# One exponential per score, eight buffers for exponentials and halves, values three double steps behind the scores, and second-layer statistics moved into the first layer's loop

## What is computed

```python
h = W.T[x] + b + positions
# first layer: 8 heads of 16 features, normalised dot products without softmax
t = layernorm(h); q, k, v = t @ w_qkv
dots = causal(q @ k.T * scale)
mu, s = mean and mean square of each causal row
h = h + ((dots - mu) * rsqrt(s + eps) * g + b) @ v @ w_out + b_out
# second layer: 2 heads of 64 features, and 8 experts of width 512
u = layernorm(layernorm(h), ln_g, ln_b)
q, k = l2norm(u @ Wq) * 8 * qn_g, l2norm(u @ Wk) * 8 * kn_g
y = softmax(causal(q @ k.T / 8)) @ (u @ Wv) @ Wo
gate = softmax(y @ gate_W + gate_b)
h = h + sum over experts e of gate[e] * (gelu(y @ W1[e] + b1[e]) @ W2[e] + b2[e])
```

## Time and profile before

| what | value |
|---|---|
| runs of the kernel before | 881.97, 884.92, 888.29 us (median 884.92) |
| the profiled execution | 880.93 us, of which the span from first to last instruction is 879.1 us |
| PE busy | 793.4 us (90% of the span) |
| DVE, ACT, POOL busy | 681.2, 489.0, 334.2 us |
| mean granted TensorE clock | 0.974 of full speed |

### The profile page before, as it was taken

How to read it: one execution, slowest core, us unless ns; L and a number is a source line. 1 busy time by engine, 2 the same in 40 slices (tenths; PEclk the granted TensorE clock), 3 DMA queues, 4 the chain that set the end, 5 groups by cost and what they waited for, 6 DMA issues and landing times.

```text
span 879.1 us, 20865 instructions
## 1 busy us (share of the span) xinstructions
PE 793.4 (90%) x8228; PEld 558.8 (64%) x8228; DVE 681.2 (77%) x1550; ACT 489.0 (56%) x1015; POOL 334.2 (38%) x379
## 2 busy tenths in 40 slices
PE   2799999998767778889899888999999999999997
PEld 1567888777533445555555556777777777777775
DVE  3668888887579755656666437899999999999997
ACT  2435555554345547668678985555555555555553
POOL 6648888666556636546557641000000000000000
PEclk9899999999889969999999999999999999999999
DMA  3201101000000000000000000000000000000000
GB/s 122 54 8 36 35 22 37 25 25 25 0 1 0 2 1 1 2 1 3 2 1 14 2 2 1 1 14 2 13 2 13 2 13 2 13 2 14 1 14 13
DMA packets 9633, 12.02 MB, mean 14 GB/s; under 512 B 1848, under 2 KB 6592, under 8 KB 9536
## 3 DMA queue, kind: packets, MB, share of 16 engines
q1 hardware_dynamic: 8512, 8.59, 3.3%
q0 software_dynamic: 1024, 2.10, 0.9%
HBM read 8.59 MB, written 2.10 MB: 12 GB/s over the span
## 4 chain that ended last, share of the span: by engine, by line
PE 70%; DVE 8%; POOL 8%; issue 7%; ACT 5%; DMA 1%; POOLq 0%; ACTq 0%; DVEq 0%
PE ps L955 68%; POOL room L360 6%; ACT room L541 2%; DVE mx L815 1%; DVE qkn L769 1%; DVE ss L754 1%; ACT room L540 1%; DMA h_all<-emb_rows,idx 1%; POOL ss L327 1%; DVE x L748 1%; PE ps L1035 1%; PE ps L963 0%; DVE ql L777 0%; DVE kl L779 0%; PE ps L983 0%
## 5 line engine op out<-in xcount | busy, mean ns | idle before, releaser
L558 ACT ACTIVATE cst<-ps,col 128x512 f32<-128x512 f32 x256 | 175.7, 688 | 162.0 <-PE ps L955 161.9
L955 PEld LDWEIGHTS ps<-arena,sq 128*128 128x128 f16 x3072 | 192.3, 98 | 61.9 <-DVE sq L939 4.1
L955 PE MATMUL ps<-arena,sq 128*128 128x128 f16 x3072 | 213.0, 219 | 0.8 <-DVE sq L939 0.7
L955 PE MATMUL ps<-y,arena 128*128 128x512 f16 x768 | 207.0, 379 | 1.3 <-DVE och L888 1.3
L939 DVE TENSOR_TENSOR sq<-cst,sq 128x512 f16<-128x512 f32 x256 | 175.6, 686 | 4.4
L360 POOL TENSOR_TENSOR room<-room 128x512 f16<-128x512 f32 (+3 forms) x119 | 118.8, 1013 | 97.9 <-ACT room L541 95.9
L815 DVE TENSOR_REDUCE mx<-ps 128x2 f32<-128x1024 f32 (+2 forms) x76 | 81.7, 1075 | 63.5 <-PE ps L955 63.3
L934 DVE CAST sq<-cst 128x512 f16<-128x512 f32 x256 | 108.6, 424 | 10.8 <-ACT cst L558 3.6
L540 ACT ACTIVATE room<-ps 128x512 f32<-128x512 f32 (+3 forms) x160 | 86.5, 541 | 46.9 <-PE ps L955 46.3
L541 ACT ACTIVATE room<-ps 128x512 f16<-128x512 f32 (+3 forms) x160 | 87.1, 545 | 0.0
L955 PEld LDWEIGHTS ps<-y,arena 128*128 128x128 f16 x768 | 64.6, 98 | 33.1 <-issue 1.8
(11 more groups left out here) (154 smaller groups left out, 1150.3 us busy)
## 6 DMA issues: line engine op xcount, KB each, us to landing
sq<-w_rows SPq DMA_DIRECT2D x16, 256.0 KB
out<-h_all SPq DMA_DIRECT2D x32, 64.0 KB, 1.6
cst<-consts SPq DMA_DIRECT2D x1, 896.0 KB
h_all<-emb_rows,idx POOLq DMA_INDIRECT x32, 4.9
cst<-consts SPq DMA_DIRECT2D x1, 398.0 KB, 3.8
c<-consts SPq DMA_DIRECT2D x1, 256.0 KB
wqkv<-w_qkv SPq DMA_DIRECT2D x1, 192.0 KB
wsm<-w_sm SPq DMA_DIRECT2D x1, 192.0 KB
```

Of the source, the lines that this page charges most:

```text
L558: a.activation(hid[:, f], ps[:, HBANK[f], :], ACT.Gelu_apprx_tanh, bias=col[:, K_B1 + k:K_B1 + k + 1], scale=1.0 / WS).then_inc(S["hid_rea ...
L955: return t_.matmul(o, l, r, start=start, stop=stop, skip_group_check=True)
```

## The change

- Stage A and B: mean and power of the second layer norm get a place for every chunk. `stats2(c-2)` (with the former `two_norms` at its end) runs on DVE in `step_a(c)` between `state_out(c, 1)` and `outputs(c-1)`; `both_norms(c-3)` runs on POOL at the head of `step_a(c)`, ahead of `coefs(c-1)`. `normed2(0)` and `normed2(1)` move into stage A's tail, the scratch `scaled` moves to the buffers `qkn` and `qk2`, `project2(0)` and `normed_T(0)` move ahead on PE. The last chunk's pieces of stage A move two steps back inside stage B.
- Stage C: ACT takes exp once into p32 for both heads, incrementing a new semaphore `s_used`, then `max_row` if there is one, then copies p32 into phi twice. `scores` waits for `s_used` instead of `p_ready`. `max_row` uses bank 5, and its guard is `bank5`, not that of the pair scores. PR = QR = 8, LAG = 3.

```diff
@@ gpsimd @@
             def step_a(c, nxt, more=2, tail=True):
+                if c >= 3:
+                    both_norms(c - 3)
                 if tail:
                     coefs(c - 1)
...
@@ vector, step_a @@
                 masked(c, 1)
                 state_out(c, 1)
+                if c >= 2:
+                    stats2(c - 2)
                 outputs(c - 1, nxt, first)
...
@@ vector, behind the loop @@
-            dve.wait_ge(S["h1_ready"], NT - 3)
-            stats2(0)
-            two_norms(0)
+            normed2(0)
             masked(NT - 2, 1)
             state_out(NT - 2, 1)
+            stats2(NT - 4)
             outputs(NT - 3, 1)
-            stats2(1)
-            two_norms(1)
+            normed2(1)
             h1_out(NT - 3)
             masked(NT - 1, 0)
             variances(NT - 2, 0)
+            sum_squares(0)
+            masked(NT - 1, 1)
+            low_v(0)
+            stats2(NT - 3)
+            outputs(NT - 2, 0)
             dve.wait_ge(S["wlow_ready"], NEARLY)
-            normed2(0)
-            masked(NT - 1, 1)
-            outputs(NT - 2, 0)
-            normed2(1)
-            stats2(2)
-            two_norms(2)
-            h1_out(NT - 2)
-            sum_squares(0)
-            low_v(0)
...
@@ vector, step_b @@
                 unit_qk(c)
+                if c == 0:
+                    h1_out(NT - 2)
+                if c == 5:
+                    h1_out(NT - 1)
...
-                if c == 3:
-                    h1_out(NT - 1)
-                if c + 3 < NT:
-                    if c + 3 >= NT - 2:
-                        dve.wait_ge(S["h1_ready"], c + 4)
-                    stats2(c + 3)
-                    two_norms(c + 3)
...
-                if c == 0:
+                if c == 1:
                     variances(NT - 1, 1)
-                if c == 1:
+                if c == 2:
+                    stats2(NT - 2)
+                if c == 3:
                     outputs(NT - 1, 1)
+                if c == 6:
+                    stats2(NT - 1)
...
@@ tensor, chunk 15 of stage A and step_b @@
+            normed_T(0)
             for b in range(B):
...
                 if b == 0:
-                    normed_T(0)
-            project2(0)
+                    project2(0)
+            normed_T(1)
...
-            normed_T(1)
             out_T(NT - 2)
+            project2(1)
             out_project(NT - 2)
-            project2(1)
...
-                if c == 1:
-                    pe.wait_ge(S["hxT_sb"], 4)
+                if c == 3:
+                    pe.wait_ge(S["hxT_sb"], 6)
                     out_T(NT - 1)
-                if c == 2:
-                    pe.wait_ge(S["hxT_sb"], 5)
+                if c == 4:
+                    pe.wait_ge(S["hxT_sb"], 7)
                     out_project(NT - 1)
...
@@ scalar, stage C @@
+                        a.activation(p32[:, i % QR, lo:], ps[:, i % 3, lo:], ACT.Exp).then_inc(S["s_used"], 1)
+                    if s in RAT:
+                        max_row(RAT[s])
+                    for i in (2 * s, 2 * s + 1):
+                        act.wait_ge(S["s_used"], i + 1)
                         if i >= PR:
                             act.wait_ge(S["pv_done"], i - PR + 1)
-                        a.activation(p32[:, i % QR, lo:], ps[:, i % 3, lo:], ACT.Exp)
-                        a.activation(phi[:, i % PR, lo:], ps[:, i % 3, lo:], ACT.Exp).then_inc(S["p_ready"], 1)
-                        if s in RAT and i == 2 * s:
-                            max_row(RAT[s])
+                        a.copy(phi[:, i % PR, lo:], p32[:, i % QR, lo:]).then_inc(S["p_ready"], 1)
...
@@ tensor, max_row and scores @@
-                if it and guard:
-                    pe.wait_ge(*guard)
+                if it:
+                    pe.wait_ge(*bank5)
...
                 if it:
-                    guard = S["mrow_sb"], it + 1
+                    bank5 = S["mrow_sb"], it + 1
...
                 if s:
-                    pe.wait_ge(S["p_ready"], 2 * s - 1)
+                    pe.wait_ge(S["s_used"], 2 * s - 1)
...
-PR, QR = 6, 6
+PR, QR = 8, 8
 WLATE = [52, 60, 66]
-LAG = 2
+LAG = 3
```

More of the change, by code:

```diff
@@ L130, in tower @@
         st2 = sb("st2", [P, 2, B, 6])
-        mv2 = [sb(f"mv2{i}", [P, B, 2]) for i in range(2)]
-        rr = [sb(f"rr{i}", [P, 2, B]) for i in range(2)]
+        mv2 = sb("mv2", [P, NT, B, 2])
+        rr = sb("rr", [P, NT, 2, B])
         x2_all = sb("x2", [P, 2, B, D])
@@ L279, in weights_low, with both_norms @@
                                 piece[:, :, 0, :], ALU.subtract).then_inc(S["wlow_ready"], 1)
+            def both_norms(c):
+                pool.wait_ge(S["stats2"], c + 1)
+                g.tensor_tensor(rr[:, c, 1], rr[:, c, 0], mhalf[:, 0:B], ALU.pow).then_inc(S["rr_ready"], 1)
             front(0, 0)
@@ L510, in max_row @@
                 act.wait_ge(S["mrow_ps"], it + 1)
-                a.copy(qm[:, it % 2], ps[:, row_bank(it), :]).then_inc(S["mrow_sb"], 1)
+                a.copy(qm[:, it % 2], ps[:, 5, :]).then_inc(S["mrow_sb"], 1)
             def out_part(m, j):
@@ L704, in masked, with stats2 @@
                                 upper.unsqueeze(1).to_broadcast([P, HA, P]), ALU.mult).then_inc(S["dt_sb"], 1)
+            def stats2(c):
+                par = c % 2
+                dve.wait_ge(S["h1_ready"], c + 1)
+                for b in range(B):
+                    last = v.bn_stats(st2[:, par, b], h_all[:, 2 * c + b, :])
+                last.then_inc(S["st2_link"], 1)
+                dve.wait_ge(S["st2_link"], c + 1)
+                for b in range(B):
+                    last = v.bn_aggr(mv2[:, c, b], st2[:, par, b])
+                last.then_inc(S["agg2"], 1)
+                dve.wait_ge(S["agg2"], c + 1)
+                v.tensor_scalar(rr[:, c, 0], mv2[:, c, :, 1], 1.0 + LN_EPS, LN_EPS * LN_EPS, ALU.mult, ALU.add
+                                ).then_inc(S["stats2"], 1)
             def step_a(c, nxt, more=2, first=False):
@@ L726, in _ @@
                     step_a(c + u, 1 - u)
[L728 to L740, removed]
-                v.tensor_scalar(rr[par][:, 0], mv2[par][:, :, 1], 1.0 + LN_EPS, LN_EPS * LN_EPS, ALU.mult, ALU.add
-                                ).then_inc(S["stats2"], 1)
             def normed2(c):
@@ L1081, in normed_T @@
                 pe.wait_ge(S["x2_ready"], c + 1)
+                if c == 0:
+                    pe.wait_ge(S["qkT_sb"], NT)
+                if c == 1:
+                    pe.wait_ge(S["sgc_ready"], 2 * NT - 2)
                 if c == 2:
@@ L1095, in project2 @@
                 pe.wait_ge(S["hxT_sb"], c + 1)
+                if c == 0:
+                    pe.wait_ge(S["qkv_sb"], 2 * NT)
                 if c == 1:
@@ L1315, in _ @@
             pe.wait_ge(S["wlow_ready"], NPIECE)
-            pe.wait_ge(S["p_ready"], 2 * NSTEP)
+            pe.wait_ge(S["s_used"], 2 * NSTEP)
             pe.wait_ge(S["sm_used"], NMAX)
```

52 lines of the change are left out of this document (24 added, 28 removed).

## The result

| | median of 12 runs | lowest to highest | profiled execution | its span |
|---|---|---|---|---|
| before | 885.3 us | 881.97 to 888.29 | 880.93 us | 879.1 us |
| after | 880.01 us | 876.24 to 885.26 | 876.45 us | 874.6 us |

The ratio after to before is 0.995, with a 95% interval of 0.9932 to 0.9968. The change saves 4.5 us in the profiled execution and 5.3 us in the medians, where the forecast was 14.5. The time lies in the range that was given, but near its end: about a third of the forecast gain came. The place where it is missing is stage C.

The account below looks back on a forecast made before the run. PE bounds stage A's loop and the experts, a DVE-POOL ring stage B, waits for ACT hold PE in C. 0 + 6 + 5 + 3.5 + 0 = 14.5 us off 880.93 gives 866.4, median 870; own range 864 to 876, outer 860 to 881.

Parts of the forecast that it names:

- Statistics into stage A: Stage A: the added statistics on DVE and power on POOL fit idle gaps, so they cost 0 us.
- Passage and ring: Passage A to B and stage B's DVE-POOL loop: earlier first `unit_qk`, then 3.89 us a chunk; gain 6 us, bounds 0 to 9.
- the 1.4 us taken off for the clock: Stage B: 1.4 us off the 7.4 us gain, for one stretch with PE's clock at half rate.
- One exponential and `s_used`: Stage C: `scores` waits for one ACT instruction instead of two; gain 5 us, bounds 0 to 7.
- nothing waits for the remainders: Stage C: POOL and DVE begin remainders later, but three double steps between scores and values cover the 0.485 us.
- The sign that the prediction set for being wrong: Listed as showing the forecast wrong, among others: a stage C as long as before, 234 us.
- 2.7 us were forecast: Last 14 full double steps of stage C: ACT becomes the next bound, gain 0.19 us each, 2.7 us.
- `max_row` in bank 5: Stage C: PE's 4.2 us of waits for the copy of the row maxima go; gain 3.5 us, bounds 0 to 4.2.
- What it took off for `out_part` 1: Stage C: `out_part` 1 now waits for the maxima's copy for three items; 0.2 us off for each.
- Eight buffers and LAG: Stage C: buffers cover the new order's cost, and `head_out` moves one double step; 0 us, bounds -2.5 to 2.5.
- The rival that stage C does not gain: Stage C: early scores only reach the next wait sooner, so 5 and 3.5 us vanish; 879 us, chance 0.13.

Follow-up runs that it names:

- e1: New stages A and B of the change, with stage C as in the kernel before: 876.49 us, ratio 0.9933 to the kernel before.
- e9: e1 plus only the single exponential with its copy and the scores' wait on `s_used`: 883.49 us, ratio 0.9989 to the kernel before.
- e11: e1 plus only the row maximum's result in bank 5: 870.22 us, ratio 0.9848 to the kernel before.
- e13: e11 plus only the single exponential and its copy (the diff of e9): 877.5 us, ratio 0.9932 to the kernel before.
- e3: The changed kernel, but DVE takes the first remainder of a shared double step and POOL the second: 873.11 us, ratio 0.9903 to the kernel before.
- e4: The changed kernel with DVE's gate part one double step earlier: 871.58 us, ratio 0.9866 to the kernel before.
- e7: The changed kernel with DVE taking the first remainder and its gate part one double step earlier: 871.63 us, ratio 0.9861 to the kernel before.
- e6: The changed kernel with the row maximum's result back in bank 3: 882.56 us, ratio 0.9983 to the kernel before.
- e5: e1 with eight buffers and LAG = 3, two exponentials kept: 880.54 us, ratio 0.9955 to the kernel before.

## Why the prediction was right and wrong

*Statistics into stage A: 0.* Right; the cover held, by 0.04 us in the loop chunk above, and the loop keeps 11.9 us a chunk.

*Passage and ring: 6.* Right, and by its own steps: first `unit_qk` at 225.16 (forecast 225.4), `h1_out(14)` at 229.11 (229), `unit_qk(7)` at 262.26 (261.4, before the 1.4 us taken off for the clock), 3.90 us a chunk behind it (3.89). e1 gives 5.9 us for it alone.

*One exponential and `s_used`: 5.* This is the step that failed, and in sign: it costs 5.0 us without bank 5 (e1 to e9) and 7.4 us with it (e11 to e13). The part of it that was worked out from rows was right: ACT allows a double step of 2.0 us at the end (forecast 2.03), in the ACT timeline after:

```profile
518.26 1.19 ACT L549 CAST room<-room 128x512 f16<-128x512 f32 x2
519.29 1.14 ACT L542 ACTIVATE room<-ps 128x512 f32<-128x512 f32 x2
520.26 1.20 ACT L549 CAST room<-room 128x512 f16<-128x512 f32 x2
```

and of the 7.0 us of waits 1.2 are left. What failed is the sentence that nothing waits for the remainders. It looked at `values` alone, and followed only the time at which the first high half is ready, 0.485 us later. The second one then comes 0.5 us behind the first instead of 1 us, DVE's subtraction falls into POOL's, and the gate and `head_out`, which stand behind it in DVE's list, are late for a PE that comes earlier; three double steps help `values`, and not these. The sign that the prediction set for being wrong came with it, a stage C of 234 us; but e1, with the old stage C, has 233.8, so that it does not tell the two apart.

That the edit costs time is shown by e9 and e13, and that DVE's order is the cause by e3, e4 and e7: at the end of stage C, where 2.7 us were forecast, the changed kernel loses 1.5 us, and e4 and e7 gain 2.7 and 3.1. Of the loss from e11 to e13, in their profiled executions, 1.5 us (7.3 less 5.8) is waiting and 5.5 us is clock. The mean clock of all the runs is lower too (0.969 in e13, 0.978 in e11), but most of the half clock does not stand behind the gate's wait, and what ties it to the edit stays open. So does why e7, with the single exponential, is not faster than e11: in the profiled executions PE stands idle less in stage C (26.8 us in e7, 28.2 in e11), but at a lower clock (over all runs 0.971 and 0.978).

*`max_row` in bank 5: 3.5.* Right in mechanism: the waits for the copy go in every pair. The size was measured with 2.9 us (e6 to the changed kernel), 5.0 (e9 to e13) and 7.5 (e1 to e11). Where it is over the 4.2 us of waits, the profile shows the excess as clock. The prediction had no term for the clock here, so what lies above 3.5 is luck. What it took off for `out_part` 1 came as 0.2 us in e11; the changed kernel has 2.2 us at the guard of bank 5 instead, which it did not name.

*Eight buffers and LAG: 0.* Right within its bounds: 2.0 us slower in the pair e1 and e5, 1.6 from e13 to the changed kernel (0.9932 to 0.995), each within overlapping intervals.

Put together from one line of runs, e1, e11, e13 and the changed kernel: 5.9 + 7.5 - 7.4 - 1.6 = 4.4 us, which is the 0.5% measured. They are differences along one chain, so that the sum has to come out; it is no check on them. The rival that stage C does not gain named the time well (879 us) and half of the reason, `head_out`; the copy is not slower than 0.53 us (two exponentials and two copies take 2.00 us), and the waits for `row_max` fell.

## What to carry to other kernels

An edit that lets one engine finish two results closer together changes which instructions of the next engines run side by side; look in the rows for pairs on POOL and DVE that read SBUF, and for what stands behind them in DVE's list, before a saving on the first engine is counted. Waits for one engine that are taken away can come back as waits for the next with nearly the same sum, as in this change (30.7 us in stage C before, 31.5 after); they need not, as e11 shows, where 4.2 us went and next to nothing came. A change of several edits should be timed edit by edit: the kernel with only the new passage and bank 5 (0.9848) beats the whole change (0.995), and the three edits of stage C that the title names are not in it.

## What the runs showed of the hardware that was not expected

A DVE product of 128x32 took 0.19 us at 508.17 before, between two POOL subtractions, and 1.16 us when it began 0.04 us behind a POOL subtraction of 1.15 us. DVE's subtraction of 128x512 ended 0.55 or 0.56 us after POOL's, whether it began 0.48 us behind it (1.23 us long) or 0.94 (0.77 us long). In e3, where it began ahead of POOL's, it took 0.69.

Near the start of stage C the granted clock was 0.50 for 17 us in the kernel before and after. Windows of 17 us there have 0.70 in e1, 0.90 in e13 and 1.00 in e11; a value between 0.50 and 1.00 is a mean of the two levels, 1.2 and 2.4 GHz. Added up over windows of 0.5 us, the time at half clock from the last `unit_qk` to the first GELU is 17.1 us before, 20.5 after, 17.1 in e1, 17.1 in e13, 20.5 in e7 and 3.4 in e11. PE's list in e1 and e11 is the same but for the bank of the row maxima and its guard, and the waits of PE from 255 to 345 us sum to 20.6 and 20.5 us (with more of the list done by then in e11). In these executions the clock was worth as much as the waits, and none of these runs shows what decides it.
